# Reordering the first and the last tile of each layer in a transformer kernel's ScalarE, VectorE and TensorE lists

## The reference

```python
x = x + layernorm(local_attention_8_wide_heads(layernorm(x)))      # first block, once
y = layernorm(x)
for i in range(6):                                                 # DEPTH
    y = attn_layer(shift_tokens(y), Wqkv[i], qs[i], ks[i], Wo[i]) + y
    y = ffn_layer(shift_tokens(y), g[i], b[i], W1[i], b1[i], W2[i], b2[i]) + y
x = x + layernorm(y)

def attn_layer(x, Wqkv, qs, ksc, Wo):          # 16 heads of 64, windows of 32
    q, k, v = split(x @ Wqkv)                  # 128 -> 3 x 1024
    q, k = l2norm(q) * qs, l2norm(k) * ksc
    q, k = rotary(q) * scale, rotary(k) / scale
    sim = q . k * 8, keys of the own and the previous window, 0 <= i - j <= 32
    return softmax(sim) @ v @ Wo               # 1024 -> 128

def ffn_layer(x, g, bln, W1, b1, W2, b2):
    xn = layernorm(x) * g + bln
    a, gate = split(xn @ W1 + b1)              # 341 each
    return a * gelu(gate) @ W2 + b2
```

## Time and profile before

| | |
|---|---|
| median of 3 runs | 1922.57 us (1919.14 to 1923.04) |
| the profiled execution | 1918.69 us |
| its span in the profile | 1916.9 us |
| mean granted clock of TensorE | 0.976 of full speed |

### The profile page before, as it was taken

How to read it: one execution, slowest core, us unless ns; L and a number is a source line. 1 busy time by engine, 2 the same in 40 slices (tenths; PEclk the granted TensorE clock), 3 DMA queues, 4 the chain that set the end, 5 groups by cost and what they waited for, 6 DMA issues and landing times. The chain is left out here.

```text
span 1916.9 us, 92788 instructions
## 1 busy us (share of the span) xinstructions
PE 1767.0 (92%) x33712; PEld 1321.4 (69%) x33712; DVE 1454.2 (76%) x4213; ACT 1494.4 (78%) x5600; POOL 1405.4 (73%) x2347
## 2 busy tenths in 40 slices
PE   7996999989999989999989999989999989999987
PEld 4664777764777764777764777764777764777763
DVE  5886888857888857888857788867788867788866
ACT  5884888875888875888875888875888875888882
POOL 4325888876888866888875888875888875888851
PEclk9997999999999999999999999999999999999998
DMA  4001333222333221333221323221323221223210
GB/s 132 14 15 30 98 75 76 67 50 55 97 76 74 67 50 46 105 75 75 67 49 49 100 71 79 68 50 45 105 69 78 71 49 41 72 68 76 75 47 22
DMA packets 135264, 125.89 MB, mean 66 GB/s; under 512 B 18097, under 2 KB 133137, under 8 KB 134161
## 3 DMA queue, kind: packets, MB, share of 16 engines
q1 hardware_dynamic: 135056, 123.06, 25.1%
HBM read 19.85 MB, written 1.05 MB: 11 GB/s over the span
## 5 line engine op out<-in xcount | busy, mean ns | idle before, releaser
L392 POOL TENSOR_TENSOR tsum<-tc_,ts_ 128x512 f32<-128x512 f32 x384 | 490.9, 1279 | 76.6 <-DVE ts_ L956 55.7
L602 ACT ACTIVATE prob<-bank,nmax 128x64 f32<-128x64 f32 x1536 | 465.5, 331 | 16.3 <-DVE nmax L905 15.6
L947 DVE TENSOR_REDUCE n<-nat 128x8 f32<-128x512 f32 x384 | 262.5, 684 | 197.5 <-ACT nat L619 193.2
L421 POOL TENSOR_TENSOR w_nat<-tsum,rn 128x512 f32<-128x512 f32 x384 | 397.0, 1044 | 16.0
L619 ACT ACTIVATE nat<-bank 128x512 f32<-128x512 f32 x384 | 239.2, 624 | 149.6 <-PE bank L1363 148.4
L602 ACT ACTIVATION_READ_ACCUMULATOR prob<-bank,nmax 128x1 f32 x1536 | 344.6, 224 | 0.0
L1361 PE MATMUL bank<-w_hi,xs 128*128 128x512 f32 x576 | 277.4, 482 | 55.7 <-DVE ts_ L956 53.3
L956 DVE TENSOR_TENSOR ts_<-bank,ropeL 128x256 f32<-128x256 f32 x768 | 286.6, 416 | 0.0
L951 DVE TENSOR_TENSOR tc_<-bank,ropeL 128x512 f32<-128x512 f32 x384 | 261.5, 681 | 0.0
L1368 PE MATMUL bank<-idf,w_nat 128*128 128x128 f32 x1536 | 239.0, 278 | 12.2 <-POOL w_nat L421 10.7
L1363 PE MATMUL bank<-w_hi,xs_lo 128*128 128x512 f32 x576 | 232.3, 403 | 0.0
(11 more groups left out here) (137 smaller groups left out, 3490.7 us busy)
## 6 DMA issues: line engine op xcount, KB each, us to landing
vspace<-v_nat SPq DMA_DIRECT2D x576, 128.0 KB
vspace<-v_nat SPq DMA_DIRECT2D x382, 64.0 KB, 2.0
nat<-w_qkv SPq DMA_DIRECT2D x5, 1536.0 KB
wo<-w_o SPq DMA_DIRECT2D x6, 512.0 KB, 4.0
w<-w SPq DMA_DIRECT2D x6, 341.0 KB, 3.0
shared<-w_qkv SPq DMA_DIRECT2D x1, 1536.0 KB
w<-w SPq DMA_DIRECT2D x6, 192.0 KB, 3.0
x_nat<-x SPq DMA_DIRECT2D x4, 256.0 KB, 3.7
```

The source lines that it names most:

```text
L392: nc.gpsimd.tensor_tensor(tsum[:, r, :], tc_[:, r, :], ts_[:, r, :], ALU.add).then_inc(sum_ready, 1)
L421: nc.gpsimd.tensor_tensor(w_nat[:, r, :].rearrange("p (h d) -> p h d", d=D), tsum[:, r, :].rearrange("p (h d) -> p h d", d=D), rn[:, r * 8 ...
L602: last = nc.scalar.activation(probs[:, slot * SEEN:(slot + 1) * SEEN], SB[b][:, i * SEEN:(i + 1) * SEEN], ACT.Exp, bias=nmax[:, p, 8 * G + ...
L947: nc.vector.tensor_reduce(n2[:, r, :, 0], sq[:, r, :].rearrange(heads3, d=D), AX.X, ALU.add).then_inc(n2_ready, 1)
```

## The change

In `start`, part 5, ScalarE takes two squares of tile 1 ahead of the copies of tile 2's input. VectorE's rest of that input leaves `start`, part 6, and goes into the first tile, behind the third rotary step. In the first tile ScalarE copies the third part of the heads (`heads_T(t, p, 2, 6)`) ahead of all exponentials and squares (`square(t + 1, 2)`) between the two groups of them; TensorE transposes the first half's probabilities ahead of projection steps 4 and 5 instead of behind them. In the last tile ScalarE's last copy of keys goes between the first two groups of exponentials, and its fourth group of exponentials ahead of `normed_T(0)`. The last transpose of outputs goes to bank 4 and waits for the first copy out of that bank instead of `normed_T(1)`. No instruction is added or removed.

```diff
--- before.py
+++ after.py
@@ -699,9 +699,9 @@
                     heads_T(t0, 0, 1, 4)
                     values(t0, 0, 1)
                 if part == 5:
-                    copy_input(2, 0)
                     square(t0 + 1, 0)
                     square(t0 + 1, 1)
+                    copy_input(2, 0)
 
             def layer(l, last):
                 t0 = l * TILES
@@ -710,14 +710,16 @@
                     if closing:
                         return tile_closing(t, p)
                     before_closing = isinstance(n, int) and n == TILES - 2
+                    if opening:
+
+                        heads_T(t, p, 2, 6)
                     exps(t, p, 0, 0)
-                    if not opening:
+                    if opening:
+                        square(t + 1, 2)
+                    else:
                         values(t + 1, 1 - p, 0)
                     exps(t, p, 0, 1)
                     if opening:
-
-                        heads_T(t, p, 2, 6)
-                        square(t + 1, 2)
                         heads_T(t, p, 3, 4)
                         seed(t + 1, 0)
                         values(t + 1, 1 - p, 0)
@@ -748,17 +750,19 @@
                         seed(t + 2, 0)
                     if before_closing:
                         shifted(l, 1)
-                    heads_T(t + 1, 1 - p, 3, 4)
+                    else:
+                        heads_T(t + 1, 1 - p, 3, 4)
 
                 def tile_closing(t, p):
                     exps(t, p, 0, 0)
+                    heads_T(t, p, 3, 4)
                     exps(t, p, 0, 1)
                     heads_out_T(t - 1, 0, 6)
                     probs_out(t, 0, 4)
                     heads_out_T(t - 1, 1, 6)
                     exps(t, p, 1, 0)
+                    exps(t, p, 1, 1)
                     normed_T(0)
-                    exps(t, p, 1, 1)
                     probs_out(t, 1, 4)
 
                 def normed_T(s):
@@ -785,7 +789,7 @@
                     gate(0, 0)
                     heads_out_T(t, 0, 4)
                     normed_T(1)
-                    heads_out_T(t, 1, 6)
+                    heads_out_T(t, 1, 4)
                 tiles(eng, tile, close, t0)
 
                 for s in range(SUPERS):
@@ -1043,7 +1047,6 @@
                 if part == 5:
                     rotary(t0, 0, 3, True)
                 if part == 6:
-                    input_rest(t0 + 2, 2, 0)
                     rotary(t0 + 1, 1, 0)
 
             def final_moments(g):
@@ -1103,6 +1106,8 @@
                         rotary(t + 1, n + 1, 1)
                     if not closing:
                         rotary(t + 1, n + 1, 2)
+                    if opening:
+                        input_rest(t + 2, n + 2, p)
                     if closing:
                         norm_stats(0)
                     if not opening:
@@ -1489,16 +1494,16 @@
                         eng.wait_ge(tp_free, t * 4 + 3)
                         transpose_out(t - 1, 0, 6)
                         weigh_values(t - 1, 1 - p, 1)
+                    if opening:
+                        eng.wait_ge(tp_free, t * 4 + 3)
+                        transpose_probs(t, 0, 6)
                     project(t + 1, 1 - p, 4)
                     project(t + 1, 1 - p, 5)
                     if not opening:
                         eng.wait_ge(tp_free, t * 4 + 4)
                         transpose_out(t - 1, 1, 4)
-                    if opening:
-                        eng.wait_ge(tp_free, t * 4 + 3)
-                    else:
                         eng.wait_ge(ot_evac, t * 2 - 1)
-                    transpose_probs(t, 0, 6)
+                        transpose_probs(t, 0, 6)
                     scores(t, n, p, 1)
                     if not opening:
                         project_out(t - 1, 0)
@@ -1550,8 +1555,8 @@
                     transpose_out(t, 0, 4)
                     eng.wait_ge(f_xnT, l * SUPERS + 1)
                     transpose_normed(1)
-                    eng.wait_ge(f_xnT, l * SUPERS + 2)
-                    transpose_out(t, 1, 6)
+                    eng.wait_ge(ot_evac, t * 2 + 1)
+                    transpose_out(t, 1, 4)
                     project_out(t, 0)
                     project_out(t, 1)
                 eng.wait_ge(wo_loaded, (l + 1) * 16)
```

## The result

| | before | changed |
|---|---|---|
| median | 1921.19 us (4 runs, 1919.14 to 1923.04) | 1899.2 us (4 runs, 1897.38 to 1900.29) |
| ratio | | 0.9892 (95% interval 0.9876 to 0.9908) |
| the profiled execution | 1918.69 us | 1898.36 us |
| its span | 1916.9 us | 1896.5 us |
| mean granted clock | 0.976 | 0.985 |

The change saves 22.0 us. Each entry is a difference of two starts, in us, for layers 1 to 6.

The account below looks back on a forecast made before the run. TensorE, busy 92% of the span, was taken as the bound. Last tile 20.1 + seed 3.7 + lead 2.1 - clock falls 3.6 = 22.3 us; 1922.6 - 22.3 = 1900.3 us, range 1893 to 1910.

Parts of the forecast that it names:

- Last tile, exponentials and norm: Last tile: exponentials move into ScalarE's idle time before xnT, so the first gate projection starts 1.67 us earlier per layer.
- The doubt about the table load: Last tile, Gelu table: 1.28 us by trace, covered; at the skill's 2.66 us the gain would be 2.4 us smaller.
- Last tile, the bank: Last tile: second transpose of outputs waits for the first oT copy instead of xnT(1), saving 0.66 us per layer.
- Last tile, the clock: Last tile, before the gate: TensorE's clock no longer falls in four layers, saving 6.1 us; bounds 0 and 6.1.
- Rival 2: Clock still falls at the gate in four layers and in the first tiles too: 14.4 us gained, 1908.2 us; chance 0.12.
- Feed-forward part: Behind the last tile: its gain reaches the layer's end, since VectorE and ScalarE wait for TensorE behind the output projection.
- the seed: First tile: GpSimd's refinement no longer waits for the seed from ScalarE, 0.62 us per layer, 3.7 us in all.
- rival 4: Nothing counts, because the shift is given back in the feed-forward part: 1922.6 us; chance 0.03.
- Rival 3: First tile's hole leaves the clock at 1.2 GHz through later loop tiles: 1952.2 us with two tiles; chance 0.03.
- First tile, the lead and its price: First tile: earlier third square and transposes gain 2.1 us; a new TensorE hole costs four clock falls of 0.9, 3.6 us.
- the third of the prediction's own signs of being wrong: Across a layer's tiles: the 215 us from first to last refinement grow.
- rival 1: First tile: clock falls in all six new holes, 1902.1 us, or in none, 1896.7; both together 0.3, mostly the first.

Follow-up runs that it names:

- the experiment: Changed kernel with the last tile's fourth group of exponentials behind the first norm copy again: 1909.01 us, ratio 0.9966.
- filling the hole in the kernel before: Kernel before plus twelve unread transposes on TensorE between the last tile's normalised transposes and those of probabilities: 1909.98 us, ratio 0.9967.
- the kernel with the hole filled: Changed kernel plus twelve unread transposes on TensorE in each first tile, ahead of the wait for the heads' third part: 1894.81 us, ratio 0.9894.
- the one without the opening's moves: Changed kernel with tile 2's input copy ahead of the two squares and the input's rest ahead of the rotary step again: 1896.65 us, ratio 0.9880.
- the last tile alone: Changed kernel with `start` and the first tile as before, so only the last tile's edits remain: 1895.70 us, ratio 0.9894.
- the ScalarE list back: Changed kernel with the first tile's copy to qT and third square behind all eight exponentials again: 1896.72 us, ratio 0.9881.
- the first tile alone changed: Kernel before with only `start` and the first tile changed: 1921.95 us, ratio 1.0035.

## Why the prediction came out near, and which step of it was wrong

**Last tile, exponentials and norm: right.** Norm to first gate projection was to be 1.6 and is 1.67 or 1.68; the order is worth 1.50 a layer by the experiment (forecast 1.67). TensorE's hole of over 2 us became 0.58 rather than 0.3. The doubt about the table load is settled as the trace of before had it: the load begins at 1844.56, the Gelu at 1845.85, and the copy behind them waits 1.02 for TensorE. The Trainium skill's 2.66 us (ScalarE: Activation LUTs, What ACT_TABLE_LOAD costs) doesn't show here: the Gelu starts 1.29 behind the load's start, and the load 0.02 behind the end of the copy ahead of it.

**Last tile, the bank: right**, 0.67 for 0.66.

**Last tile, the clock: right.** 8.03 in all six layers, where 7.9 was forecast, and filling the hole in the kernel before was worth 6.2 where the clock was put at 6.1. Together with the keys (0.7, forecast 0 with a bound of 0.14 a layer) the last tile gave 19.9 us; the forecast was 20.1. Rival 2, a fall at the gate, is out.

**Feed-forward part: right.** It shrank by what the seed saved (0.69 four times and 0.36 once, forecast 0.62), and gave nothing of the last tile's gain back, so rival 4 is out. Rival 3 is out too: a fall in the changed kernel's first tiles is over in under 4 us, and the loop's tiles show 1.00.

**First tile, the lead and its price: wrong.** The prediction counted a gain of 2.1 us for the lead and a cost of 0.9 for a fall in each of four layers, a net loss of 1.5. The trace shows a loss of 6.0, and so the third of the prediction's own signs of being wrong: the 215 us from first to last refinement grew. Two terms failed. The lead was to be worth 2.1 and is worth 0.0 to 1.3; the fall was to cost 3.6 and costs 5.5, five times 1.1, which lies between the forecast of four falls and rival 1's six. The prediction also took a fall in these tiles for something new. Busy times by stretch of the kernel before, about 1.5 to 5.5 and 12.5 to 16.5 behind R, fourth layer:

```profile
1054.00:1058.00 4.00, 3.96 (x12) 2.98 (x12) 1.68 (x4) 1.60 (x4) 3.53 (x7) 0.50 0.99 334
1065.00:1069.00 4.00, 3.76 (x124) 2.97 (x109) 4.00 (x12) 3.18 (x14) 2.81 (x7) 1.00 0.02 4
```

and of the changed kernel, the same two stretches of the first layer:

```profile
188.00:192.00 4.00, 2.97 (x77) 2.08 (x75) 3.08 (x8) 3.30 (x11) 3.61 (x6) 1.00 0.82 338
199.00:203.00 4.00, 4.00 (x84) 3.09 (x72) 1.75 (x4) 1.97 (x7) 2.40 (x5) 0.72 0.00 0
```

Before, the clock was already at its lower level in every first tile, in the early stretch. There TensorE's slower passes cost little where it still has to wait for GpSimd's third part 11 us behind R. In the changed kernel's profile those falls are gone, and there are five others, behind the third part. These lie on a chain that leads to GpSimd. ScalarE in the second layer of the changed kernel:

```profile
486.13 0.60 ACT L619 ACTIVATE nat<-bank 128x512 f32<-128x512 f32 x1 [1.45 <-PE bank L1368]
486.63 0.30 ACT L624 ACTIVATE rn<-n2c,log_bias 128x16 f32<-128x16 int32 x1
```

and in the fourth layer of the kernel with the hole filled:

```profile
1049.54 0.60 ACT L619 ACTIVATE nat<-bank 128x512 f32<-128x512 f32 x1 [0.82 <-PE bank L1368]
1050.03 0.30 ACT L624 ACTIVATE rn<-n2c,log_bias 128x16 f32<-128x16 int32 x1
```

The seed stands behind a square in ScalarE's list, and the square waits for the third pass of a projection. With the slow passes the square starts 14.24 behind R, without them 13.59, and GpSimd waits 0.75 for the seed or not at all.

The price can be read from 14 profiles. In the eleven whose first tile has the change, whole or in part, 66 layers, the clock fell late in 47: first to last refinement 216.00 to 217.46, mean 216.56. In the other 19 it is 215.13 to 216.46, mean 215.47. **A late fall costs 1.1 us**, not 0.9. The three kernels with the first tile as before have no late fall in 18 layers, and a mean of 215.49. So by the means the lead itself is worth 0.0. Only four layers without a late fall have a first tile exactly as changed; their mean is 215.28, by which the lead would be worth 0.2 a layer, 1.3 in all. Neither is 2.1.

The early fall isn't free everywhere. In 7 of the 18 layers with the first tile as before the granted clock is still at its lower level 6.4 behind R. These are the layers in which GpSimd waits 0.87 or 0.88 (the second, fourth and sixth of the kernel before), and they take 215.79 in mean; the other eleven, where the fall is over by 6.3, take 215.30. So the 0.6 that the prediction read from these waits was about right (0.5), but as these layers have it, it was a price of the early fall. In the changed kernel these waits went, and the seed's waits came in their place: 0.75 to 1.47 in the five layers with a late fall, none in the fourth.

Three slips of the working change little. The terms of the third square's lead add up to 2.2 and not 2.1, and the fifth projection came 1.03 closer to R (1.7 with the seed's 0.69) and not 2.0; neither is in the sum. The four differences of the clock add up to 6.15, and the lag of TensorE behind xnT is 0.05 by its rows.

**The total.** From the first R to the end the profiled executions differ by 17.1 us (1727.17 and 1710.04); by the prediction's steps it would be 22.3 - 0.6 = 21.7. That the median came within 1.1 us of 1900.3 is therefore in part luck: the lead's gain and the falls were wrong by 4.5 us together, and 3.3 us of the profiled difference lie ahead of the first R, of which only the seed's wait (0.6) has to do with the change. The first R lies at 189.73 before and 186.46 after, but over all 14 profiles anywhere from 184.41 to 191.24, with the first block's code the same in all. The granted clock there differs between them: 0.86 before and 1.00 after from 40 to 60 us. The change made once more gave a ratio of 0.9907, some 18 us.

**The best version.** By the trace from the first R on it is the changed kernel with twelve added transposes, 1704.8 us, followed by the one without the opening's moves (1706.8), the last tile alone (1707.2) and the changed kernel (1710.0 and 1707.2 in two profiles), one execution each. The intervals of their ratios, 0.9894, 0.9880, 0.9894 and 0.9892, overlap, so no median here ranks them. All beat the kernel before. The last tile alone with the opening's moves, and fillings at both places of the first tile, were not tried.

## What to carry to other kernels

Ask of a stall not only how long it is but what stands behind it: the same drop of TensorE's clock cost next to nothing where TensorE was going to wait for GpSimd anyway, 0.5 us where it lasted too long for that, and 1.1 us where the other engines were waiting for TensorE. Pulling work forward on an engine whose next input has a fixed time only moves its idle time; test each half of such a change alone, since here the other half carried all the gain. And before pricing a new fall of the clock, look whether the stretch already has one, by the granted clock every few microseconds and not by a stage's mean.

## What was not expected of the hardware

- The same code with the same hole gives a fall in some layers and none in others. In the changed kernel five holes of 1.95 to 2.49 us have one behind them and the fourth layer's hole of 2.48 has none; with the ScalarE list back, holes of 1.09 and 1.08 have one (layers 3 and 6) and holes of 1.55 to 1.57 have none. The Trainium skill (TensorE: Matmul & The Clock Gate, HAM oscillation) tells of a kernel whose waits for DMA of about 3 to 5 us lower the clock anew each time; the holes here are shorter, so no run here shows that case. What decides between layers stays open.
- TensorE's transposes that nobody reads hold the clock: twelve (1.47 us in one row; 0.80 of idle time left behind them at the gate, 1.15 in most first tiles) removed every fall at both places. Four, tried in the first tile alone, removed none.
- With the first tile alone changed, the clock fell at the gate of all six layers, and with the exponentials back in two of six, though TensorE's hole is 2.11 us in both. Whether that comes from what was changed elsewhere isn't shown, since these are single executions and the changed kernel's own two profiles differ in the first layer.
- The fifth layer takes some 1.0 us longer in several kernels (216.46 with the hole filled, 216.24 with the last tile alone). With the hole filled the granted clock is 1.00 from its first to its last refinement, so it isn't a fall; against the fourth layer its refinements lose some 0.2 in five places of the loop. With the last tile alone, some 0.5 of it is the long early fall. The rest stays open.
